# Two attentions whose score maxima run thirteen units, in place of fifteen, in front of the exponentials

## What is computed

```python
# first attention (L0)
q  = einsum('bse,oe->bso', x, wq) + bq
qh = q.reshape(16, b, s, 8); kh = qh; vh = qh
attn = softmax(einsum('hbqd,hbkd->hbqk', qh, kh) / sqrt(128), axis=-1)
out  = einsum('hbqk,hbkd->hbqd', attn, vh)

# second attention (L3), keys in 4 blocks of 128
s_blk = einsum('bhqd,bhkd->bhqk', q, k_blk) * 8 ** -0.5
m = max(s_blk, axis=-1); e = exp(s_blk - m)
num = num + einsum('bhqk,bhkd->bhqd', e, v_blk); den = den + sum(e)
```

## Time and profile before

| | us |
|---|---|
| median of 3 runs | 1940.92 |
| lowest and highest run | 1937.31, 1942.98 |
| the profiled execution | 1938.45 |
| its span in the profile | 1936.6 |

### The profile page before, as it was taken

The page is one execution under the profiler, slowest core; times in us unless marked ns, Lnnn a source line. Parts: engine busy times, 40 slices in busy tenths (PEclk is TensorE's granted clock), DMA queues, the critical chain, the costliest instruction groups (busy, mean ns, idle before and its releaser), DMA issues.

```text
span 1936.6 us, 25616 instructions
## 1 busy us (share of the span) xinstructions
PE 1573.3 (81%) x9076; PEld 1067.2 (55%) x9076; DVE 1295.2 (67%) x3055; ACT 1013.9 (52%) x1782; POOL 566.1 (29%) x536
## 2 busy tenths in 40 slices
PE   4997499998799699639989976985983699995694
PEld 3776133333577488417878865984982222223693
DVE  5687388884688633585435966695874588875583
ACT  2553177787455355225537623751663278882372
POOL 3674100001377100113026837554005000002203
PEclk9998589999799799869989987996996599997797
DMA  4111814400221200101000010003553703300473
GB/s 147 60 52 36 126 23 50 50 1 1 66 75 37 66 1 1 57 7 42 1 1 11 1 44 1 1 1 98 155 160 99 123 9 43 50 1 9 135 213 94
DMA packets 113642, 104.04 MB, mean 54 GB/s; under 512 B 17570, under 2 KB 98546, under 8 KB 113268
## 3 DMA queue, kind: packets, MB, share of 16 engines
q1 hardware_dynamic: 110674, 97.41, 21.3%
q0 software_dynamic: 2048, 4.20, 0.7%
q10 hardware_dynamic: 792, 0.79, 0.2%
HBM read 88.60 MB, written 13.76 MB: 53 GB/s over the span
## 4 chain that ended last, share of the span: by engine, by line
PE 48%; DVE 29%; POOL 8%; issue 6%; ACT 5%; DMA 3%; POOLq 1%; SPq 0%; DVEq 0%; another core or an unknown queue 0%; ACTq 0%
PE bank L93 9%; PE bank L95 8%; PE bank L94 8%; PE bank L2296 5%; PE bank L2311 5%; PE bank L2268 4%; DVE x L1471 4%; DVE mx L2481 4%; DVE xn L213 3%; PE bank L2275 2%; DVE st L195 2%; DVE hl L1927 1%; DVE q L687 1%; POOL yg L1963 1%; DMA qq<-in_key_rows 1%
## 5 line engine op out<-in xcount | busy, mean ns | idle before, releaser
L2481 DVE TENSOR_REDUCE mx<-bank 128x1 f32<-128x512 f32 (+1 forms) x512 | 323.7, 681 | 72.0 <-PE bank L2268 69.3
L2410 ACT ACTIVATE e<-bank 128x512 f32<-128x512 f32 x512 | 276.8, 597 | 62.4 <-PE bank L2296 59.6
L2296 PE MATMUL bank<-qq,kk 99*128 99x512 bf16 (+1 forms) x512 | 160.9, 394 | 2.2 <-ACT e L2410 1.8
L1487 POOL TENSOR_TENSOR midl<-mid,midh 128x512 fp32r<-128x512 f32 (+1 forms) x96 | 132.0, 1382 | 76.2 <-ACT midh L1407 76.0
L2548 POOL TENSOR_TENSOR osb<-ot,rc 128x128 f32<-128x128 f32 x32 | 13.0, 407 | 471.4 <-DVE rc L2506 471.4
L1011 DVE TENSOR_TENSOR hl<-q,hh 128x512 fp32r<-128x512 f32 x64 | 49.4, 772 | 122.7 <-ACT hh L981 100.7
L185 PE MATMUL bank<-cf,xn 128*128 128x128 f32 x192 | 44.2, 373 | 105.6 <-DVE xn L213 93.2
L205 POOL TENSOR_SCALAR rs<-mv 128x4 f32<-128x4 f32 x52 | 13.1, 252 | 391.9 <-DVE mv L199 391.8
L93 PE MATMUL bank<-wdh,midh 128*128 128x256 f32 (+1 forms) x384 | 111.8, 291 | 10.9 <-DVE x L1471 10.5
L240 ACT COPY xT<-bank 128x512 f32<-128x512 f32 x44 | 25.8, 586 | 181.1 <-PE bank L185 180.8
L2394 ACT CAST qq<-bank 3x512 bf16<-3x512 f32 (+1 forms) x128 | 74.1, 579 | 72.7 <-PE bank L2275 69.4
(11 more groups left out here) (393 smaller groups left out, 4613.7 us busy)
## 6 DMA issues: line engine op xcount, KB each, us to landing
w<-in_L_ffn_W SPq DMA_DIRECT2D x30, 512.0 KB
w<-in_L_ffn_W SPq DMA_DIRECT2D x30, 256.0 KB
qq<-scratch SPq DMA_DIRECT2D x19, 384.0 KB
w<-in_L_ffn_w_kernel SPq DMA_DIRECT2D x16, 344.0 KB
w<-in_L_ffn_w_kernel SPq DMA_DIRECT2D x16, 320.0 KB
wo<-in_L_ffn_wo_kernel SPq DMA_DIRECT2D x16, 320.0 KB
w<-in_L_ffn_W SPq DMA_DIRECT2D x30, 128.0 KB
sorted_y<-y SPq DMA_DIRECT2D x30, 128.0 KB, 1.8
```

The source lines that it names most:

```text
L1487: e.tensor_tensor(l[0:fn, o], mid[i % 2][0:fn, o], h[0:fn, o].bitcast(F32), ALU.subtract).then_inc(*l2_m_lo.tick(n, i, f))
L2296: e.matmul(b_bank(t, u, j), keys(kk[0:K], t, b)[:, k * 128:(k + 1) * 128], queries(qq[0:K], t, b), start=True, stop=True).then_inc(*at_b.t ...
L2410: e.activation(er[u][:, j * 512:(j + 1) * 512], b_bank(t, u, j), ACT.Exp, bias=0.0, scale=scale).then_inc(*at_e.tick(n, t, u, j))
L2481: e.tensor_reduce(mxa[t % 3][:, o:o + nkb], bank[place_a["a", t, u, j]].rearrange("p (k n) -> p k n", k=nkb), X, ALU.max).then_inc(*at_max ...
```

## The change

AHEAD is 13, so the score pairs run two units less in front of the exponent pairs. The split of head t+1 and the last of its maxima then stand at u = 2 of head t. The four placings of head t+1 stand at u = 4, 5, 6 and 7, one in each unit of the second half. Sums, values, close and everything else keep their places. No instruction is added or removed.

```diff
-            AHEAD = 15
+            AHEAD = 13
@@
-                if u % 2 == 1 and t + 1 < 16:
-                    order.append(("place", t + 1, u // 2))
+                if u >= 4 and t + 1 < 16:
+                    order.append(("place", t + 1, u - 4))
```

## The result

The changed kernel takes 1974.1 us (median of 4 runs, 1971.84 to 1979.2), the kernel before 1941.95 in the runs beside it (4 runs, 1937.31 to 1943.88). The ratio is 1.0163, with a 95% interval of 1.0137 to 1.019: slower by about 32 us. The profiled execution took 1971.84 us, 33.4 more than that of before.

A forecast was written before the change was run, and what follows sets the result against it. PE was taken as the bound, DVE having a tenth to spare. Second attention +13.1 and first +19.4 gave +31.5 to +32.5 on the profiled 1938.45, 1970.5; with the runs' median 2.5 higher, the middle, 1972 us, range 1951 to 1988.

The forecast's parts named there:

- Part 1: First placing of a head no longer waits for the split: 0.32 us a head disappears.
- Part 2: Split and close together on DVE hold u = 4's second score matmul: +1.12 us a head, +14.6 in the second attention.
- Part 3: Second-half placings, each waiting for the copy before: costs nothing, 0.12 us to spare; first attention's values wait +0.3.
- First attention: Same hold plus the values' waits in the first attention: plain heads 15.07 us against 13.63, sum over heads +20.2.
- Part 4: Ends: -2.4 us ahead of each attention; head 14 +0.9 in the second, +1.6 in the first; head 0 nothing.
- Lump hidden: Rival: the hold of PE by split and close lies under other work, faster than before, 1931 us; chance 0.05.
- ACT second: Rival: ACT becomes a second bound, second-half placings each wait 0.3 us, +24, so 1996 us; chance 0.09.
- The hold is smaller: Rival: PE is held for half of the time, 0.8 us less in 26 heads, 1951 us; chance 0.11.
- The clock falls: Rival: PE's clock falls and its stream of 12.86 us a head doubles in 26 heads, about 2260 us; chance 0.01.

The follow-up runs named there:

- e6: The kernel before with AHEAD 16 in place of 15, placings at the old places: 1935.15 us, ratio 0.9966.
- e3: The changed kernel with AHEAD 14 in place of 13, late placings kept: 1970.26 us, ratio 1.0151 to the kernel before.
- e4: The changed kernel with the fourth sum, and with it the close, at u = 1 in place of u = 2: 1985.89 us, ratio 1.0234.
- e2: The changed kernel with AHEAD 15 in place of 13, late placings kept: 1944.05 us, ratio 1.0018 to the kernel before.
- e1: The change in the second attention alone, the first attention as in the kernel before: 1945.74 us against 1939.36, ratio 1.0031.
- e10: e8's kernel with three filler matmuls on PE in front of each held score pair: 1990.49 us, ratio 1.0242 to the kernel before.
- e8: The changed kernel with each close's reciprocal done three times on DVE in place of once: 2024.51 us, ratio 1.0446 to the kernel before.
- e9: The changed kernel with three filler matmuls on PE in front of each held score pair: 1973.47 us, ratio 1.0163 to the kernel before.

## Why the prediction was right, and where it was off

The forecast was 1972, and 1974.1 was measured. The range had it, and slower was right by mechanism, but the closeness is in part luck. The second attention came out 6.6 us below its sum, the first 4.0 above it, and 3.6 of the profiled difference lie in code that the change doesn't touch and the forecast had at nothing.

**Part 1, the placings' wait goes:** right. The first placing waits for nothing at 1631.29. What the 0.32 is worth alone shows in e6: 13.02 a head, by the working 13.04.

**Part 2, the lump:** the mechanism was right, in place and in kind (the second score matmul of u = 4, held for DVE `mx`, once a head), and e3, e4 and e8 confirm it; e2, where the chain begins one unit earlier, is held for only 0.24. The size was not: +0.67 a head and not +1.12. Two parts of the sum were too large, by 0.18 and 0.27. The chain is 5.39 us (1625.58 to 1630.97) and not 5.57: four maxima behind one another took 2.52 (1626.00 to 1628.52) and not 2.58, the close 0.91 and not 0.93, and the 0.10 for the weight load was counted on top though the matmul starts 0.68 behind the maximum's start, weight load included (1630.29 to 1630.97). The rest of the head, from the held matmul to the next score pair of u = 1, is 8.64 and not 8.91. A placing directly in front of a sum does not cost its 0.32: the sum starts 0.02 behind it, and both together take 1.18 (1631.29 to 1632.47) where I had added 0.32 and 1.00. This happens twice a head. 13 x 0.67 = 8.7, where the sum had 14.6.

**Part 3, placings one after another:** right. In the second attention none waits for ACT in heads 1 to 13 (one does in head 14, 0.70 us at 1773.64, where the score pairs between the placings have ended), and the values of the first wait 0.39 where 0.3 was forecast; e2 shows this wait alone, 0.34 a plain head.

```profile
289.19 0.57 PE L2283 MATMUL bank<-cb,kk 99*128 99x32 bf16 x16 [0.39 <-ACT qq L2394]
```

**First attention:** from the split of head 2 to that of head 15 it grew by 24.2 (190.9 to 215.1), where the sum had 20.2. The order's own cost was over-sized as in part 2: plain heads +1.11 in place of +1.44, heads with a key copy 15.35 - 13.77 = +1.58 in place of +1.9, and a head with `turn` and `out` together with the next one 33.28 - 31.20 = +2.1 in place of +2.9. That leaves 16.1 to 18.6 for the order and 5.6 to 8.1 for the clock, which the sum had at nothing.

**Part 4, ends:** about right, -2.2 in the second attention (6.5 less 8.7; forecast -1.5) and -0.8 in the first (23.4 less 24.2; forecast -0.8).

**The rivals.** "Lump hidden" and "ACT second" did not come. "The hold is smaller" was true in size and not for its reason: start to start the matmul is held 1.37 (1630.97 less 1629.38 and 0.22) and not 1.62, and the head is 0.45 shorter than forecast, against the 0.8 of this rival. "The clock falls" is the step that failed in kind. I gave it 0.01, and only in one form, the whole of both attentions at 1.2 GHz. It came as four stretches of 3.5 to 7 us, worth 1.4 to 2.5 us each, behind single waits of PE. The evidence for leaving it out was that holds of 0.5 and 1.08 us left the clock alone in one trace. The change made holds of 1.10 to 2.97 in the first attention, most of them outside of what those rows cover, and one trace was too little even for what they cover: a wait of 1.08 was followed by a stretch in the changed kernel, and holds of 0.79 and 0.59 in e1. By the Trainium skill, Perfetto Trace Analysis, Matmul Optimizations, the engine scales its power with utilization and wants matmuls back to back; e10 against e8 agrees with it, 34 us less with three matmuls more in each hold. The rule on banks of the Trainium skill, Perfetto Trace Analysis, Optimizing Tensor Performance, is not enough by itself here: three banks rotate, and yet PE was held 1.22 us in heads 1 to 13 of the second attention, as the chain on DVE took 5.39 us against 4.02 of PE's own stream (1625.58 to 1629.38, and 0.22 for the first of the two matmuls).

## What to carry to other kernels

When one engine's work is moved later, write down both chains between the same two points, what the other engine must do and what this one does meanwhile, and look in which gap the moved work used to lie: here a head of the second attention lasts 13.02 us with the split a unit ahead of its first placing (e6), 13.36 with the first placing waiting for it, and 14.03 once it stands behind DVE's idle time. Gaps that this opens on TensorE can cost twice, the second time as a low granted clock behind them, so price them from the first, and use the granted clock by windows before explaining why one head is longer than its like. Misses that cancel are found only if every term has its own measured row, and the time of untouched code is compared as well.

## What was not expected of the hardware

- **Short stretches at 1.2 GHz behind idle time of 0.6 to 3 us,** worth 1.4 to 2.5 us each in the changed kernel. In the second attention idle time of 1.79 in every head brought eight (e8), and with matmuls in it, 0.70 left, none (e10). But 1.22 in every head brought none in 13 heads, and 1.13 in every head brought three, in each fourth head (e4). Behind 1.08 us at `out` the clock fell once in the changed kernel and once in e9 and never in the kernel before. So the length of one wait alone doesn't decide it. What else does stays open.
- **Matmuls into different rows of PSUM run side by side.** This reading rests on starts and sums of time; no run varied the rows. A placing (4 matmuls into rows 96 and up) and a sum (32 rows each) take 1.18 us together and 0.32 and 1.00 apart, the sum starting 0.02 behind the placing. Likewise three filler matmuls took 1.00 (1630.06 to 1631.06), exactly what a sum's four take, and not the 0.75 that was expected.
- **Doing more can be faster:** e10 against e8, 26 x 3 matmuls more and 34 us less.
